# Expert weights in two ring parts, and operands placed 192 bytes (mod 256) apart

## What is computed

```python
def _swiglu(x, gu_w, dn_w):
    gate, up = jnp.split(x @ gu_w, 2, axis=-1)
    gate = jnp.clip(gate, -10.0, 10.0)
    return jax.nn.silu(gate) * up @ dn_w
...
out = jnp.zeros_like(xf)
for e in range(E):
    out = out + comb[:, e:e + 1] * _swiglu(xn, gate_up_w[e], down_w[e])
```

## Time and profile before

| | us |
|---|---|
| median of 3 executions | 1178.47 (1177.61 to 1181.77) |
| the profiled execution | 1188.74 |
| its span, first to last instruction | 1186.7 |
| TensorE busy in the span | 1097.3 |

### The profile page before, as it was taken

How to read it: one execution, slowest core, us unless ns; L and a number is a source line. 1 busy time by engine, 2 the same in 40 slices (tenths; PEclk the granted TensorE clock), 3 DMA queues, 4 the chain that set the end, 5 groups by cost and what they waited for, 6 DMA issues and landing times.

```text
span 1186.7 us, 23315 instructions
## 1 busy us (share of the span) xinstructions
PE 1097.3 (92%) x7492; PEld 976.9 (82%) x7492; DVE 832.7 (70%) x2113; ACT 654.8 (55%) x1325; POOL 303.0 (26%) x358
## 2 busy tenths in 40 slices
PE   3989999999989998999999999999999999999940
PEld 2765776677767666999999999999999999999940
DVE  5986898897878766666666666666666666666645
ACT  6768866777665364444444444445444544444425
POOL 1142132633441534121221122122112211221224
PEclk9999999998989999999999999999999999999975
DMA  8655765973664789522331245555922367211239
GB/s 298 230 191 185 251 216 189 322 244 137 215 229 151 245 276 348 182 59 56 63 71 18 36 127 189 198 163 179 384 34 36 75 208 230 36 28 25 36 86 215
DMA packets 96617, 191.70 MB, mean 162 GB/s; under 512 B 8768, under 2 KB 59456, under 8 KB 96576
## 3 DMA queue, kind: packets, MB, share of 16 engines
q1 hardware_dynamic: 80160, 170.38, 41.7%
q0 software_dynamic: 16416, 20.85, 10.2%
HBM read 295.62 MB, written 86.41 MB: 322 GB/s over the span
## 4 chain that ended last, share of the span: by engine, by line
PE 80%; DVE 7%; issue 4%; DMA 3%; SPq 2%; ACT 2%; POOL 2%; ACTq 0%; DVEq 0%; POOLq 0%
PE bank L1337 12%; PE bank L464 12%; PE bank L1339 12%; PE bank L1338 12%; PE bank L1350 6%; PE bank L1348 6%; PE bank L1349 6%; PE bank L458 4%; PE bank L459 4%; PE bank L460 4%; PE bank L1325 1%; DVE xr L1478 1%; DVE a_cum L869 1%; DMA e_raw<-w_e 1%; POOL xs_scratch L1144 1%
## 5 line engine op out<-in xcount | busy, mean ns | idle before, releaser
L1337 PE MATMUL bank<-h_hi,w_both 128*128 128x256 f32 x936 | 268.2, 287 | 0.1
L1287 POOL DMA_INDIRECT acc_scratch<-cv,ids x78 | 126.9, 1627 | 551.4 <-DVE cv L1426 510.8
L1447 DVE TENSOR_SCALAR cv<-bank 128x256 f32<-128x256 f32 x312 | 132.1, 423 | 191.4 <-PE bank L1339 191.4
L1338 PE MATMUL bank<-h_hi,w_both 128*128 128x256 f32 x936 | 261.0, 279 | 0.0
L1339 PE MATMUL bank<-h_hi,w_both 128*128 128x256 f32 x936 | 260.9, 279 | 0.0
L1397 ACT ACTIVATE cv<-cv 128x256 f32<-128x256 f32 x312 | 130.3, 418 | 231.8 <-DVE cv L1447 231.7
L1389 ACT ACTIVATE h_lo<-cv 128x256 fp32r<-128x256 f32 x312 | 130.0, 417 | 114.8 <-DVE cv L1454 114.8
L1338 PEld LDWEIGHTS bank<-h_hi,w_both 128*128 128x128 f32 x936 | 176.6, 189 | 0.0
L1337 PEld LDWEIGHTS bank<-h_hi,w_both 128*128 128x128 f32 x936 | 176.4, 188 | 0.4 <-issue 0.3
L1339 PEld LDWEIGHTS bank<-h_hi,w_both 128*128 128x128 f32 x936 | 176.6, 189 | 0.0
L1454 DVE TENSOR_TENSOR cv<-bank,cv 128x256 f32<-128x256 f32 x312 | 132.4, 424 | 47.5 <-ACT cv L1397 39.2
(11 more groups left out here) (227 smaller groups left out, 2395.6 us busy)
## 6 DMA issues: line engine op xcount, KB each, us to landing
w_both<-w_split SPq DMA_DIRECT2D x228, 768.0 KB
xs_hi<-w_split SPq DMA_DIRECT2D x38, 768.0 KB
xs_lo<-w_split SPq DMA_DIRECT2D x38, 768.0 KB
e_raw<-w_e SPq DMA_DIRECT2D x64, 384.0 KB
w_split<-e_high SPq DMA_DIRECT2D x64, 384.0 KB
w_split<-e_raw SPq DMA_DIRECT2D x64, 384.0 KB
u<-xs_scratch SPq DMA_DIRECT2D x40, 260.0 KB
x_in<-x SPq DMA_DIRECT2D x8, 512.0 KB
```

The lines of the kernel that those rows point to most:

```text
L1337: nc.tensor.matmul(out, e_hi[f][:, cols], xg_hi[:, par, c, :], start=c == 0, stop=False)
L1338: nc.tensor.matmul(out, e_hi[f][:, cols], xg_lo[:, par, c, :], start=False, stop=False)
L1447: nc.vector.tensor_scalar(gate[:, f % 4, :], gu_ps[f % 2][:, 0:G], CLIP, -CLIP, ALU.min, ALU.max).then_inc(clipped, 1)
```

## The change

The ring is cut in two. A chunk's gate-and-up weights (high and low, 2 x 512 words) stand in `w_gu[f]`, its down weights (2 x 256 words) in `w_d[f]`, which begins 16 words further. Each chunk is loaded by two DMAs from the same place in DRAM, the first in runs of 2,048 bytes, the second in runs of 1,024 (where it was one run of 6,144), and each adds 16 to `loaded[f]`, for which TensorE now waits at 32 per group. `w_both` is 64 words longer, so all tiles behind it move by 256 bytes. The places of the operands inside a stretch of 256 bytes, in bytes, worked out from the code and the tiles' starts:

| | before | after |
|---|---|---|
| gate-up: stationary weights / moving rows | 64 / 0 | 64 / 128 |
| down: stationary hidden / moving weights | 128 / 64 | 64 / 128 |
| stationary minus the moving one before it, inside gate-up | 64 | 192 |
| the same, inside down | 64 | 192 |
| first down product after gate-up | 128 | 192 |
| first gate-up product after down | 0 | 192 |

The raw rows (`rows`, in `u`) move by 64 bytes too. The mixer's matmuls keep their places inside 256 bytes.

```diff
@@ -54,7 +54,8 @@
-X_AT, H_AT = 48, 16
+X_AT, H_AT, D_AT, R_AT = 16, 0, 16, 16
+GUW = 2 * 4 * P
@@ -69,7 +70,7 @@
         def sem(name):
...
-        w_both = sb("w_both", [P, 2 * W_COLS], F32R)
+        w_both = sb("w_both", [P, 2 * W_COLS + HALF // 8], F32R)
@@ -207,7 +208,11 @@
-        ring = [w_both[:, f * 2 * CW:(f + 1) * 2 * CW] for f in range(FC - 2)] + [flat(v[:, :, :])[:, 0:2 * CW] for v in (xs_hi, xs_lo)]
+        xs_flat = [flat(v[:, :, :]) for v in (xs_hi, xs_lo)]
+        d_base = (FC - 2) * GUW + D_AT
+        gu_ring = [w_both[:, f * GUW:(f + 1) * GUW] for f in range(FC - 2)] + [v[:, 0:GUW] for v in xs_flat]
+        d_ring = [w_both[:, d_base + f * 2 * D:d_base + (f + 1) * 2 * D] for f in range(FC - 2)]
+        d_ring += [v[:, GUW + D_AT:GUW + D_AT + 2 * D] for v in xs_flat]
@@ -215,8 +220,8 @@
-        homes = (ring, quad(u_flat[:, 0:2 * GT * ROW]), quad(x_home[0]), quad(x_home[1]),
-                 u_flat[:, 2 * GT * ROW:2 * GT * ROW + DC * G].rearrange("p (c g) -> p c g", g=G),
+        homes = (gu_ring, d_ring, quad(u_flat[:, R_AT:R_AT + 2 * GT * ROW]), quad(x_home[0]), quad(x_home[1]),
+                 u_flat[:, R_AT + 2 * GT * ROW:R_AT + 2 * GT * ROW + DC * G].rearrange("p (c g) -> p c g", g=G),
@@ -1180,8 +1185,9 @@
     LAG = 3
-    w, rows, xg_hi, xg_lo, xg_f, gate, hg_hi, hg_lo, y, acc, x1, small = homes
-    e_hi, e_lo = [chunk[:, 0:CW] for chunk in w], [chunk[:, CW:2 * CW] for chunk in w]
+    w_gu, w_d, rows, xg_hi, xg_lo, xg_f, gate, hg_hi, hg_lo, y, acc, x1, small = homes
+    gu_hi, gu_lo = [part[:, 0:4 * P] for part in w_gu], [part[:, 4 * P:8 * P] for part in w_gu]
+    d_hi, d_lo = [part[:, 0:D] for part in w_d], [part[:, D:2 * D] for part in w_d]
@@ -1220,9 +1226,17 @@
+        halves = lambda v: v.bitcast(F32).rearrange("p (h c) -> p h c", h=2)
+
+        def chunk_parts(e, f):
+            split = w_s[e, f, :, :].rearrange("p (h c) -> p h c", h=2)
+            return split[:, :, 0:4 * P], split[:, :, 4 * P:CW]
+
         def load_chunk(g, f, e, new):
...
-            sp.dma_start(w[f].bitcast(F32), w_s[e, f, :, :], cond=new).then_inc(loaded[f], 16)
+            gu, d = chunk_parts(e, f)
+            sp.dma_start(halves(w_gu[f]), gu, cond=new).then_inc(loaded[f], 16)
+            sp.dma_start(halves(w_d[f]), d, cond=new).then_inc(loaded[f], 16)
@@ -1243,7 +1257,9 @@
         def first_weights():
...
-                sp.dma_start(w[f].bitcast(F32), w_s[e, f, :, :]).then_inc(loaded[f], 16)
+                gu, d = chunk_parts(e, f)
+                sp.dma_start(halves(w_gu[f]), gu).then_inc(loaded[f], 16)
+                sp.dma_start(halves(w_d[f]), d).then_inc(loaded[f], 16)
@@ -1326,7 +1342,7 @@
         def gate_up(g, par, f):
-            pe.wait_ge(loaded[f], 16 if isinstance(g, int) and g == 0 else g * 16)
+            pe.wait_ge(loaded[f], 32 if isinstance(g, int) and g == 0 else g * 32)
@@ -1334,9 +1350,9 @@
                 for c in range(DC):
...
-                    nc.tensor.matmul(out, e_hi[f][:, cols], xg_hi[:, par, c, :], start=c == 0, stop=False)
-                    nc.tensor.matmul(out, e_hi[f][:, cols], xg_lo[:, par, c, :], start=False, stop=False)
-                    i = nc.tensor.matmul(out, e_lo[f][:, cols], xg_hi[:, par, c, :], start=False, stop=c == DC - 1)
+                    nc.tensor.matmul(out, gu_hi[f][:, cols], xg_hi[:, par, c, :], start=c == 0, stop=False)
+                    nc.tensor.matmul(out, gu_hi[f][:, cols], xg_lo[:, par, c, :], start=False, stop=False)
+                    i = nc.tensor.matmul(out, gu_lo[f][:, cols], xg_hi[:, par, c, :], start=False, stop=c == DC - 1)
@@ -1345,9 +1361,9 @@
             for t in range(GT):
...
-                nc.tensor.matmul(out, hg_hi[:, f % 4, toks], e_hi[f][:, 4 * P:CW], start=f == 0, stop=False)
-                nc.tensor.matmul(out, hg_hi[:, f % 4, toks], e_lo[f][:, 4 * P:CW], start=False, stop=False)
-                i = nc.tensor.matmul(out, hg_lo[:, f % 4, toks], e_hi[f][:, 4 * P:CW], start=False, stop=f == FC - 1)
+                nc.tensor.matmul(out, hg_hi[:, f % 4, toks], d_hi[f], start=f == 0, stop=False)
+                nc.tensor.matmul(out, hg_hi[:, f % 4, toks], d_lo[f], start=False, stop=False)
+                i = nc.tensor.matmul(out, hg_lo[:, f % 4, toks], d_hi[f], start=False, stop=f == FC - 1)
```

## The result

The changed kernel takes 1192.86 us (median of 4 runs, 1189.78 to 1196.40), the kernel before 1180.12 us beside it (4 runs, 1177.61 to 1182.15): a ratio of 1.0106, 95% interval 1.0079 to 1.0134. It is slower by about 1%, some 13 us, where 14 us less were forecast. The rival "the worse level" (1189 us, up to 1201) is what happened.

A forecast was written before the change was run, and what follows sets the result against it. TensorE's product pitch was taken to bound the expert stage. From the median of 1178.47 us, 17.3 us less for pitch and 3 us more for loads gave -14.3 us, 1164 us; range 1138 to 1192 us.

The forecast's parts named there:

- the worse level: Rival: all expert products go at 118 to 120 ns, as down does now; 1189 us, up to 1201; chance 0.21.
- What bounds the kernel: Expert stage: TensorE is full at clock 1.00 and others wait for it, so pitch changes count over 5,616 products.
- Distance, down to the good level: Expert products: every pitch at 113.3 ns, a group 16.77 us in place of 17.21, 17.3 us less in 39 groups.
- The premise that 192 is to be judged as a distance: Expert products: addresses plausibly matter; 192 bytes, unseen there, was bounded by pitches from the 109 ns floor to 120 ns.
- The distance does nothing: Rival: order or absolute place sets the pitch levels, which stay; only the loads cost, 3 us; 1181 us; chance 0.13.
- The loads: Ring loads at expert changes: shorter runs delay chunks, 0.4 us on each of 7 changes, 3 us in all.
- The sum: Whole kernel: -17.3 us of pitch and +3 of loads give -14.3 us, 1164 us against the median of 1178.47.
- SyncE: hidden: SyncE's queue: eight more issues per group cost 1.7 us, 3.9 at an expert change, all hidden in its wait for `down`.
- The mixer: untouched: Mixer before the expert stage: operands keep their places inside 256 bytes, so its cost was put at nothing.
- a sign against its premise: A mixer that ends at another time than now would make the premise wrong that it isn't touched.
- what the prediction left open: Profiled execution of 1188.74 us against the median of 1178.47: the 10 us weren't explained; the same saving was assumed in both.

## Why the prediction was wrong

**What bounds the kernel: right.** The differences between the stages of these kernels are read in the pitch of TensorE's products, times their number, and in its waits: 0.40 x 19 = 7.6 us and 1.6 us for the change, 21.8 us in the loop between the two kernels without transposes.

**"Distance, down to the good level": the step that failed.** The prediction took every pitch at 113.3 ns, 16.77 us a group, and 17.3 us less. Measured: every pitch at 117.8, a group 17.40 us, 7.6 us more. Its two reasons were that 113 ns was the nearest level shown for these products, and that the change takes away the distance of 0 ahead of the slow pitches. The first didn't tell the two levels apart: 118 was shown as well, in the down products and behind transposes. The second was half true. At 0 a product does cost 120.0 ns, and its removal did remove the three slow pitches. But the first four gate-up pitches of a plain chunk came to 472 ns on average, where four at 117.8 are 471: that gain is 1 ns. And in the kernel before, gate-up came down to 113.3 ns behind the step over the 0, in all 228 plain chunks. The change took away the disturbance and with it the way in, and left as entries the transposes, which lead to 117.8 ns at these places: 73 entries of 73 without a wait. The good level itself isn't out of reach there, as the three chunks in a row with the identity at 192 show. That the 0 was the entry is inferred from where the levels change in the timelines; no run kept the places inside and took the 0 away alone. It isn't an entry at any places: with 192 inside, the same step led to 117.8 ns in all 228 plain chunks.

**The premise that 192 is to be judged as a distance: too narrow.** "192 bytes occurs nowhere among these products, and must be bounded" was right, and the bounds held: the rival's 6 x 2.12 + 2 x 2.34 = 17.40 us is the measured group to 0.01 us. What was wrong was the choice between the bounds. It was made by nearness of a level. The rows had a better sign: down had its moving operand off the start of a 256-byte stretch and never left 118 ns; after the change gate-up has too. The prediction wrote this down for the rival and gave it 0.21. Even this isn't a rule, as 64 bytes with the moving operand at 64 has 219 good chunks.

**"The distance does nothing": wrong.** 0 bytes costs 120.0 ns for every product, 128 a mean of 118.6, and 64 without transposes 113.3. The Trainium skill (TensorE: Matmul & The Clock Gate, Step-by-step: what each phase is for) says that loading the next weights doesn't take read bandwidth from the running product. By that, the places of the two operands shouldn't change the pitch. The runs show that places do, for whatever reason: with the same instructions, 21.8 us of the loop lie between two sets of places.

**The loads: right in size, not in form.** 3 us were forecast as 0.4 us at each of 7 changes. With the old places the split costs 1.0027, 3 us on 1181.87 (0.4 to 6.0 by the interval). It comes as a few larger waits: three for `w_both<-w_split` with 1.3 us in all, and two of them only with 0.8 us in the changed kernel, up to 0.8 us each. From 990 to 992 us the ring load moves 373 GB/s, where it was 430, and its end came later: the share from 996 to 998 us is 0.91, it was 0.59. A later issue may have a part in this: the last DMA of the ring is issued at 991.78 us now, at 991.25 before, though TensorE is 0.3 us ahead; no run parts rate and issue. The Trainium skill (DMA: Bandwidth & Descriptors, Specifications) has line rate from 512 bytes on. The trace disagrees: in runs of 2,048 and 1,024 bytes this window moved 13% less than in runs of 6,144, with the DMA engines full in both.

**The sum.** 7.6 us of pitch and about 3 of loads are 10.6 us, 0.9%; the measured ratio is 1.0079 to 1.0134. The two terms cover it. Of the profiled execution's 9.2 us, 7.6 are pitch and 1.6 waits.

**SyncE: hidden, but mis-sized.** 0.21 us for one more skipped issue and 60 us less of its wait were forecast. The wait for `down` fell by 152.6 us, from 348.7:

```profile
SPq L1238 <- PE bank L1366: 196.1, 175, 1.6
```

Two things were mis-sized. The DMA instruction costs 125 ns when skipped in the new form and not the 73 of the earlier trace rows; not skipped, 0.55 us and not 0.36. And the forecast's 133 + 73 ns left out a move of 29 ns in each issue and some 0.12 us between its instructions. The DMA's row, with count, ns min/median/max, first and last start:

```profile
L1238 SPq DMA_DIRECT2D w_both<-w_split x196: 125/125/629, 560.8 to 1125.8; - x196
```

and two skipped issues of one chunk in the timeline of the queue:

```profile
966.97 0.12 SPq L1238 DMA_DIRECT2D w_both<-w_split  x1
967.38 0.12 SPq L1239 DMA_DIRECT2D w_both<-w_split  x1
```

The second starts 0.41 us after the first, twice what was forecast for the added issue, and the first's own DMA instruction is 0.05 us longer than before. That is about 0.46 us for each of the some 260 chunks of this stretch, 120 of the 153 us. Where the transfers aren't skipped the issues take more, and I haven't parted the rest. SyncE still waits, so none of it reaches TensorE by this way.

**The mixer: untouched, though it ended at another time.** The prediction called this a sign against its premise. It wasn't: the commonest pitch there is the same, the granted clock was 0.98 in place of 0.96, and the end moves between executions by more than that. The clock also bears on what the prediction left open, the 10 us between the profiled execution and the median of before: the execution of 1188.74 us had a mean clock of 0.966, and 23 of those 24 executions had a higher one.

## What to carry to other kernels

Where matmuls run back to back, read the pitch of each run of them, and where in the stream it changes. If one shape shows two pitches at one clock, the places of the operands in SBUF are a parameter to be tried by running, since no single distance told good from bad here, and removing a visible disturbance can remove what led to the good level. Price a layout change at each level that the trace shows for the same products, and don't choose the better one for being near.

## What the runs showed of the hardware

- A float32r product of 128 x 128 weights and 256 columns at clock 1.00 has no single cost. Where one distance holds for all products (stationary operand's start from that of the moving one before it, mod 256), its pitch is 120.0 ns at 0, 118.6 on average at 128, in a cycle of five, and 113.3 or 117.8 at 64 and 192. 0 and 128 were run at one set of places each.
- The two levels at 64 and at 192 hold themselves. Without transposes in the stream the good one lasted for up to 144 chunks of 18 products and the other for up to 169; in the kernels with one distance it changed only behind transposes or at a stop of the stream, of 0.06 us or more. A wait can change it or leave it. None of the runs came below 113.3 ns, where transposes reach 109.
- Places that no product reads go with other patterns of the level: those of the identity (182 or 233 good chunks) and of the rows (222 or 167, 182 or 156) in the transposes.
- The time of one kernel goes with the granted clock: 1173.72 us at 0.979 and 1186.89 us at 0.968, both of the kernel before.
- Still open: why there are two levels, and what picks one at an entry. The runs say where it is picked. A rule that gives all of the counts (3, 102, 156, 167, 182, 219, 222, 233) from the places was not found.
- A skipped DMA issue costs SyncE 125 ns in the form with two dimensions of runs, and 73 in the plain one.
